# Sixteen 128-column products of the maxima made eight of 256 columns, and three steps of the even units reordered, in a two-layer cross-attention kernel on one core

## The reference

```python
def layer(x, ctx, Wq, Wk, Wv, Wo, bo):            # x (32,256,320), ctx (32,77,512)
    q, k, v = heads(x @ Wq), heads(ctx @ Wk), heads(ctx @ Wv)   # 20 heads of 16
    p = softmax(einsum('bhsd,bhld->bhsl', q, k) / sqrt(16))     # over the 77 keys
    return merge(einsum('bhsl,bhld->bhsd', p, v)) @ Wo + bo + x
x = layer(layer(x, ctx, L0...), ctx, L1...)
```

## Time and profile before

| what | value |
|---|---|
| times of three runs | 942.4, 946.02, 947.88 us; median 946.02 us |
| the profiled execution's own time | 937.91 us |
| its span (first to last instruction) | 936.1 us |
| TensorE busy, share of the span | 901.5 us, 96% |
| VectorE, ScalarE, GpSimd busy | 73%, 58%, 43% |
| mean granted TensorE clock | 0.998 of full |

### The profile page before, as it was taken

One profiled execution on the slowest core, in us unless ns is written; L12 is line 12 of the kernel. 1 busy time (PEld: TensorE's weight loads), 2 busy tenths in 40 slices (PEclk: granted clock), 3 DMA queues, 4 the chain that ended last, 5 costly groups with the idle time before them and its releaser, 6 DMA issues.

```text
span 936.1 us, 30582 instructions
## 1 busy us (share of the span) xinstructions
PE 901.5 (96%) x12766; PEld 692.7 (74%) x12766; DVE 686.5 (73%) x1223; ACT 540.1 (58%) x547; POOL 399.6 (43%) x227
## 2 busy tenths in 40 slices
PE   8899999999999999999899999999999999999897
PEld 5777877777787877777677787877878777777665
DVE  4875786866778776786867778686786868778566
ACT  4456565655556566566466556556565656656552
POOL 3424354533446254275543456354344625433323
PEclk9999999999999999999999999999999999999999
DMA  6213534545345544545455435444534544443442
GB/s 214 88 34 83 142 82 131 139 122 138 92 110 133 162 127 111 137 111 153 124 146 131 108 101 141 134 129 113 143 97 114 141 128 134 102 129 80 120 109 78
DMA packets 80537, 112.58 MB, mean 120 GB/s; under 512 B 21201, under 2 KB 37879, under 8 KB 80401
## 3 DMA queue, kind: packets, MB, share of 16 engines
q1 hardware_dynamic: 80400, 110.62, 44.1%
HBM read 60.24 MB, written 22.24 MB: 88 GB/s over the span
## 4 chain that ended last, share of the span: by engine, by line
PE 42%; DMA 20%; SPq 17%; DVE 10%; issue 6%; ACT 3%; POOL 1%; DVEq 0%; ACTq 0%; POOLq 0%
PE pR L305 16%; PE pR L430 8%; DMA X<-in_xT 7%; SPq L1387 6%; PE pA L377 5%; DMA X<-y 5%; PE pR L364 5%; DMA y<-X 4%; SPq L1394 3%; DMA out<-X 3%; SPq L1357 3%; ACT P L740 2%; PE pA L383 2%; DVE Oraw L1006 2%; SPq L1421 2%
## 5 line engine op out<-in xcount | busy, mean ns | idle before, releaser
L740 ACT ACTIVATE P<-pA 77x2048 f32<-77x2048 f32 x160 | 300.1, 1876 | 171.8 <-PE pA L383 171.5
L991 DVE TENSOR_REDUCE Mx<-pR 128x4 f32<-128x308 f32 (+1 forms) x480 | 258.8, 575 | 32.8 <-PE pR L364 29.8
L1250 POOL TENSOR_TENSOR On<-On,OS 128x1024 f32<-128x1024 f32 (+1 forms) x58 | 105.5, 1840 | 272.0 <-DMA OS<-rd 272.0
L305 PE MATMUL pR<-OS,Wo 128*128 128x512 f32 x638 | 168.9, 404 | 2.2 <-DVE OS L1047 1.4
L305 PE MATMUL pR<-XS,Wq 128*128 128x512 f32 x638 | 167.5, 402 | 2.6 <-POOL Wq L1236 1.5
L430 PE MATMUL pR<-P,VA 77*17 77x256 f32 x2480 | 157.0, 384 | 0.7 <-ACT P L740 0.3
L364 PE MATMUL pR<-KH,QH 32*128 32x154 f32 x1280 | 136.5, 292 | 19.1 <-ACT P L740 7.8
L364 PEld LDWEIGHTS pR<-KH,QH 32*128 32x128 f32 x1280 | 95.7, 184 | 78.1 <-issue 44.4
L377 PE MATMUL pA<-QH,KH 32*77 32x256 f32 x1280 | 145.1, 291 | 0.1
L305 PEld LDWEIGHTS pR<-XS,Wq 128*128 128x128 f32 x638 | 115.9, 189 | 29.4 <-POOL Wq L1236 1.9
L305 PEld LDWEIGHTS pR<-OS,Wo 128*128 128x128 f32 x638 | 114.1, 188 | 30.7 <-issue 3.8
(11 more groups left out here) (152 smaller groups left out, 1199.0 us busy)
## 6 DMA issues: line engine op xcount, KB each, us to landing
On<-Oraw SPq DMA_DIRECT2D x248, 64.0 KB, 2.6
OS<-rd SPq DMA_DIRECT2D x58, 256.0 KB
C<-in_cT SPq DMA_DIRECT2D x16, 616.0 KB, 7.9
X<-in_xT SPq DMA_DIRECT2D x16, 512.0 KB
y<-X SPq DMA_DIRECT2D x16, 512.0 KB, 4.1
X<-y SPq DMA_DIRECT2D x16, 512.0 KB
out<-X SPq DMA_DIRECT2D x15, 512.0 KB, 4.1
X<-in_xT SPq DMA_DIRECT2D x16, 256.0 KB
```

The costliest lines, as they stand in the source:

```text
L305: f = pe.matmul(p[:, :], W[:, k, c0:c0 + 128], S[:, s, :], start=(i == 0), stop=(i == len(pairs) - 1))
L740: act.activation(P[0:L, i % PR, :, :], pA[0:L, :, :], ACT.Exp, scale=float(D) ** -0.5).then_inc(p_done, 1)
L991: dve.tensor_reduce(Mx[:, :].rearrange("p (j i) -> p j i", j=4)[:, j:j + banks, i:i + 4], pR[:, bank:bank + banks, 0:2 * LK].rearrange("p ...
L1250: pool.tensor_tensor(On[rows, blocks, :], On[rows, blocks, :], recips(u, part).bitcast(F32), ALU.mult).then_inc(o_mul, 1)
```

## The change

There are three edits. The products of `less_maxima` take 256 columns instead of 128: `Mx` holds the two blocks of 128 tokens of a batch side by side (128 x 2 x 128), `max_rows` makes two transposes into one bank and copies 256 columns, `neg` has 10 columns, the reduction writes its outputs into the two blocks, and `run` has 10 steps instead of 12. In the even units ScalarE takes the exponential S(u, 1) ahead of `split_x(u + 2)`. And in all even units but 30, TensorE does K(w, 2) ahead of Q(u + 2, 2), with the half copies of ScalarE and the half sums of VectorE in the same order.

```diff
-NI = 20
+NI = 10
-        Mx = sb("Mx", [128, 128])
-        Mt = sb("Mt", [128, 128], F32R)
+        Mx = sb("Mx", [128, 2, 128])
+        Mt = sb("Mt", [128, 2 * 128], F32R)
@@ TensorE
-                pe.transpose(p[:, 0:128], Mx[:, :], ident[:, :]).then_inc(mt_pe, 1)
+                pe.transpose(p[:, 0:128], Mx[:, 0, :], ident[:, :])
+                pe.transpose(p[:, 128:256], Mx[:, 1, :], ident[:, :]).then_inc(mt_pe, 1)
-                def less_maxima(t, j):
-                    i = 8 * ms + 2 * t + p if ms < 2 else 16 + 2 * (t % 2) + t // 2
-                    return pe.matmul(pA[0:L, j, t * 128:t * 128 + 128], neg[32 * j:32 * j + 32, i:i + 1].broadcast_to([32, L]),
+                def less_maxima(h, j):
+                    i = 4 * ms + 2 * h + p if ms < 2 else 8 + h
+                    return pe.matmul(pA[0:L, j, h * SQ:h * SQ + SQ], neg[32 * j:32 * j + 32, i:i + 1].broadcast_to([32, L]),
                                      Mt[32 * j:32 * j + 32, :], start=False, stop=True, skip_group_check=True)
-                for step in range(12):
+                for step in range(10):
-                    if u is not None and step == 11:
+                    if u is not None and step == 9:
                         g.then_inc(s_pe, 1)
-                    if n is not None and step == 10:
+                    if n is not None and step == 8:
                         take_pair(second, 1)
-                        if 6 <= step < 10 and u is not None:
+                        if 6 <= step < 8 and u is not None:
                             less_maxima(step - 6, j)
-                        if step >= 10 and n is not None:
-                            f = tokens_by_keys(step - 10, j)
+                        if step >= 8 and n is not None:
+                            f = tokens_by_keys(step - 8, j)
+                    K(w, 2, 0)
                     Q(u + 2, 2, 3)
-                    K(w, 2, 0)
@@ ScalarE
-                act.activation(Mt[:, :], psum(slot["MX", u])[:, 0:128], ACT.Copy).then_inc(mt_copied, 1)
+                act.activation(Mt[:, :], psum(slot["MX", u])[:, 0:256], ACT.Copy).then_inc(mt_copied, 1)
+                        S(u, 1)
                         split_x(u + 2)
-                        S(u, 1)
+                    k_half_copy(w)
                     q_half_copy(u + 2)
-                    k_half_copy(w)
@@ VectorE
-                i = 8 * m + 4 * b
+                i = 4 * m + 2 * b
-                dve.tensor_reduce(Mx[:, :].rearrange("p (j i) -> p j i", j=4)[:, j:j + banks, i:i + 4],
-                                  pR[:, bank:bank + banks, 0:2 * LK].rearrange("p j (a k) -> p j a k", k=L),
+                dve.tensor_reduce(Mx[:, :, :].rearrange("p t (j i) -> p j t i", j=4)[:, j:j + banks, :, i:i + 2],
+                                  pR[:, bank:bank + banks, 0:2 * LK].rearrange("p j (t a k) -> p j t a k", t=2, k=L),
+                    k_sum(w)
                     q_sum(u + 2)
-                    k_sum(w)
```

More of the change, by code:

```diff
@@ L406, in run @@
                             keys_by_tokens(step, j)
-                        if 6 <= step < 10 and u is not None:
+                        if 6 <= step < 8 and u is not None:
                             less_maxima(step - 6, j)
-                        if step >= 10 and n is not None:
-                            f = tokens_by_keys(step - 10, j)
-                    if n is not None and step == 11:
+                        if step >= 8 and n is not None:
+                            f = tokens_by_keys(step - 8, j)
+                    if n is not None and step == 9:
                         f.then_inc(x_pe, 1)
@@ L1263, in _ @@
                 pool.memset(ones[:, p, D - D * p:2 * D - D * p], 0.0)
-            pool.memset(Mx[:, :], 0.0).then_inc(pads, 1)
+            pool.memset(Mx[:, :, :], 0.0).then_inc(pads, 1)
             pool.wait_ge(d_c, 16)
```

## The result

The changed kernel is slower by 0.65%. Its median is 949.12 us over 20 runs (944.02 to 954.98), that of the kernel before 944.36 us over 20 runs on the same chip (938.33 to 949.14); the ratio is 1.0065, with a 95% interval of 1.0043 to 1.0088. The forecast was 0.66% faster (939.8 of 946.0) in a range of 931 to 947, so the sign was missed, and the range by 2 us at its upper end. Forecast and measured change, -6.2 and +4.8 us, lie 11 us apart.

What follows compares the result with a forecast made beforehand. TensorE's own work was taken as the bound, busy 901.5 of 936.1 us. Wider products -4.5, transpose +2.4, the orders -2.5 and clock -1.6 sum to -6.2: 939.8 of 946.0 us, range 931 to 947.

Steps and rivals of the forecast that it cites:

- K ahead of Q: Even units: K(w, 2), 1.2 us, fills TensorE's 1.0 us wait for GpSimd before Q; moving half copies and sums costs nothing.
- the clock: TensorE's granted clock, 0.58 of full after a 1.42 us wait, recovers if that wait goes: -1.6 us (0 to -1.6).
- Wider products: Stages on TensorE: 256-column products save 0.035 us a stage in about 130 of 160, -4.5 us (0 to -7.4).
- The second transpose: TensorE: one more transpose costs 0.15 us, uncovered in 16 odd units, +2.4 us (+1.3 to +6.2).
- Exponential ahead of the rounding: ScalarE, even units: waits before stage 2 go; seven units gain 4.4 us, five others lose 0.8 in all.
- GpSimd's end: Unit 12: GpSimd's work on x ends at 388.77, before K ends at 388.93, so Q does not wait; margin 0.2 us.
- The wait of 1.75 us: In the unit with this wait there is no V(w, 2) to fill; TensorE waits for GpSimd, some 0.3 us stays won.
- Q of unit 14: GpSimd also forms Wq's rest; the chain starts 2.0 us later, K fills 1.2: +0.8 us (0 to +2.0).
- -4.4 - 0.3 + 0.8: Exponential first: seven units' waits -4.4 us, the 1.75 us wait's unit -0.3, five units with early x +0.8.
- The parts did not cancel: Rival: short products cost only their columns and a transpose 0.20 us in every unit; +2 us, about 946; chance 0.25.
- the slower rival: VectorE's reductions, output cut into two blocks, cost 0.15 us more each and become the bound; about 952; chance 0.08.
- Late transfers: Rival: x lands later in timed runs, waits twice as large, the reorder wins 5 us more; 934.5; chance 0.15.

Runs made afterwards that it cites:

- e3: Kernel before with only K(w, 2) moved ahead of Q(u + 2, 2), in the old banks; 961.41 us, 1.0157 of the kernel before.
- e4: Changed kernel with only the banks exchanged, K(w, 2) in bank 3 and Q(u + 2, 2) in bank 0; 937.45 us, 0.9899 of the kernel before.
- e9: Kernel before with only K(w, 2) ahead of Q(u + 2, 2) and their banks exchanged (3 and 0); 938.74 us, 0.9973 of the kernel before.
- e10: The same kernel as e4, all of the change with banks exchanged, timed again in another set; 935.39 us, 0.9935 of the kernel before.
- e5: Kernel before with only the exponential S(u, 1) ahead of the rounding of x; 961.36 us, 1.0180 of the kernel before.
- e2: Kernel before with only the wide products and their two transposes, all orders as before; 944.86 us, 0.9980 of the kernel before.
- e8: e4 with four more transposes a unit, whose results nobody reads; 941.34 us, 0.9976 of the kernel before.
- e11: Kernel before with both changes of order and the banks of K and Q exchanged, products narrow; 936.91 us, 0.9956 of the kernel before.
- e1: Changed kernel with Q(u + 2, 2) put back ahead of K(w, 2); wide products and exponential first stay; 953.53 us, 1.0086 of the kernel before.

## Why the prediction was wrong

**The step that failed** is this sentence of the part on K ahead of Q: "Moving the two half copies and half sums costs nothing: both lie beside PV and stage 3; if they came late, the maxima of stage 3 behind them would." It asked who is queued behind the half sums on VectorE, and not who waits for the bank that they free. In place of nothing the trace has 0.65 us in each even unit from 0 to 28, 9.8 us in 15 units. All that was needed stood in the code and in the earlier trace rows: bank 3 in the call of Q, the pair 2 and 3 in the call of stage 3, a copy of half a bank and two sums behind it, as V(w, 2) has them in the earlier trace rows, and only PV left between. e3 shows the wait without the other edits, and e4, e9 and e10 show it gone when Q lies in another bank.

**Its price is more than the waits.** e3 loses 17 us against e9, and its 15 waits on the half sum are 9.8 us of them. A second part is a collision. VectorE's `K_lo` of the third block comes after stage 3, and where it meets GpSimd's normalisation it is held up. In unit 12 of the changed kernel:

```profile
395.59 3.69 POOL L1252 TENSOR_TENSOR On<-On,OS 128x1024 f32<-128x1024 f32 x2 [4.78 <-DMA OS<-rd]
395.63 3.83 DVE L917 SCALAR_TENSOR_TENSOR KL<-Kt,mask,KH 128x154 fp32r<-128x154 f32 x2
...
399.38 0.79 DVE L993 TENSOR_REDUCE Mx<-pR 128x8 f32<-128x616 f32 x1
...
400.42 0.34 PE L366 MATMUL pR<-KH,QH 32*128 32x154 f32 x2 [2.06 <-DVE Mx L993]
```

The two instructions of line 917 take 2.54 and 1.37 us beside GpSimd's two of 2.40 and 1.33, where this form has a median of 0.37:

```profile
L917 DVE SCALAR_TENSOR_TENSOR KL<-Kt,mask,KH x32: 367/372/2536, 48.3 to 851.0; 128x154 fp32r<-128x154 f32 x32
```

The maxima behind them come late, and with them the banks of stage 4. GpSimd loses next to nothing: its pairs take 2.39 and 1.29 us where nothing meets them. The Trainium skill (SBUF — State Buffer, "SBUF: two separate sides") says that VectorE and GpSimd share a pair of ports under a lock held for the whole instruction, that a VectorE instruction with two inputs in SBUF needs it against a GpSimd instruction that reads SBUF, and that the one that starts second is blocked. The trace agrees: GpSimd's start first (395.59 against 395.63, 397.95 against 398.09), and each of line 917 ends 0.17 to 0.18 us after the one of line 1252 that it met.

The waits on these late maxima are 4.9 us in 3 places here and 4.7 in 4 in e3, against one of 2.0 before and none in e9 and e10 over the same stretch. They come with any delay in the middle of the unit and not with the bank wait alone: e5, which waits at Q instead, has 5.4 us in 4 places.

A third part could be the clock, which the prediction had as a gain, and here single profiles mislead. Two windows of the changed kernel, with the columns of the earlier trace rows:

```profile
458.50:468.00 9.50, 7.65 (x69) 6.12 (x62) 5.84 (x11) 4.31 (x5) 3.01 (x3) 0.64 0.28 86
904.80:917.00 12.20, 10.56 (x124) 5.79 (x125) 7.60 (x12) 4.86 (x6) 3.45 (x2) 0.63 0.23 70
```

Ahead of the first stand TensorE's waits of 1.69 us (Q in unit 14, at 451.73) and 0.65 us (bank 3, at 454.82), and within it one of 1.85. At 0.64 of full a part of the time is at 1.2 GHz: the eight products of line 306 from 463.45 on take 3.78 us, against 2.11 at full clock (425.16). By the granted clock of the records, the time at 1.2 GHz adds up to 21 us in the changed kernel's profiled execution, 25 in e3 and 24 in e5, but only 4 in that of before and 6 in e9 and in e10. That looks like a rule, but the other profiles break it: e2, without any of the new waits, has 28 us, and e4 has 14 where e10, the same kernel, has 6.

The timed runs say more, as each has its mean granted clock on record. Their mean is 0.9934 over the 20 runs of the changed kernel, and 0.9938 over the 21 runs of before in the first set (the 20 beside the changed kernel have none on record), so the clock does not explain why the change is slower. For e3 it may explain a part: 0.9895 over 6 runs against 0.9938 for before, where e9 has 0.9957 against 0.9950. A difference of 0.005 is some 9 us more at 1.2 GHz, and these cost at most half of it, some 5 us, an estimate from these means. Bank waits (9.8), late maxima (4.7) and clock (up to 5) together can make the 17 us between e3 and e9. How they divide is not shown, since no run has one without the others.

**Wider products: right mechanism, smaller.** A stage that nothing holds went from 1.367 us, the median before, to 1.32, 0.047 less. One of them, in unit 13, from its first product to the next operation:

```profile
423.84 0.34 PE L366 MATMUL pR<-KH,QH 32*128 32x154 f32 x2
...
425.16 2.11 PE L306 MATMUL pR<-XS,Wq 128*128 128x512 f32 x8
```

That is more than the 0.035 that were taken, but only in half the stages. Stages 0, 3 and 4 of the even units and 3 and 4 of the odd have it. Stage 1 of the even and stages 1 and 2 of the odd units stay at 1.39, stage 0 of the odd at 1.58: their second pair of banks is held by VectorE's `out` and `o_copy`. The "ordinary stage" of the earlier trace rows, 1.39 us, was itself a held one. So it is 80 stages times 0.047, -3.8 us, and not 130 times 0.035, -4.5. The 256-column products follow each other 0.117 apart, as expected. (The formula that the prediction took from the Trainium skill's "Back-to-back issue gap" is given there for the gap of an isolated product; for a stream in which each product has its weight load the section has about 81 ns at 128 columns, where the rows here have 0.07.)

**The second transpose: right, smaller.** In the timeline of the changed kernel:

```profile
469.07 0.27 PE L329 MATMUL pR<-ident,Mx 128*128 128x128 f32 x1
469.18 0.27 PE L330 MATMUL pR<-ident,Mx 128*128 128x128 f32 x1
469.38 0.43 PE L432 MATMUL pR<-P,VA 77*17 77x256 f32 x4
```

It costs 0.11 us and not 0.15, so 16 times 0.11 is +1.8 and not +2.4. In front of PV, where nothing waits, the next product came 0.20 us after the single transpose and comes 0.31 after the first of two. In front of V it came after 0.085 (369.44 to 369.53 before) and comes after 0.194; there the second transpose starts 0.165 after the first and V 0.03 behind it. The 0.19 of the earlier trace rows was the reading of one unit, 13, in which TensorE had just waited 0.18 us; thirteen of the fifteen places have 0.085. The two ends taken for the price, 0.08 and 0.20, enclosed it. The Trainium skill (TensorE: Matmul & The Clock Gate, "Part 4: PE-mode transpose") has about 275 ns for one inside a kernel. That agrees with how long each is in the records here (0.27), but it is not what one more costs: transposes that follow one another are 0.11 apart in e8. The net of both terms is -2.0 worked out, -1.9 in e2 (0.998) and -1.5 between e11 and e10. It was forecast as -2.1. None of the runs tells it from zero by its interval.

**Exponential ahead of the rounding, and GpSimd's end: right in the timeline.** 4.89 us after stage 1 (forecast 5.04), no wait on the exponential, GpSimd's end some 0.1 us before Q. The wait of 1.75 us was forecast to leave 0.3 of gain; in the changed kernel that place (842.32) waits 1.65 us for line 1060, so 0.1 stays. Q of unit 14 waits 1.69 against 1.50 and starts after K, as priced. In unit 0, K waits 1.03 for its bank, as priced too. e1 and e5 bear out that the exponential needs K in front: alone it costs 1.8%. What it brings with K in front is smaller than forecast: e11 and e9 differ by it alone and lie 1.8 us apart in their medians, which their intervals do not tell from nothing, where -4.4 - 0.3 + 0.8, -3.9, was worked out. In e11 2.2 us of waits ahead of stage 2 end with VectorE's `out(z, 0)` instead.

**The sum without the failed step.** e10 has every edit of the change, and only the bank numbers differ. Its ratio of 0.9935 is -6.1 us of 941.5; the forecast for the change was -6.2. Of this, the two orders alone (e11) give 0.9956, -4.1, where -2.5 and -1.6 were worked out. The interval of each is some 2 us to either side, so this agreement is better than the data can vouch for, and in part it is luck. The clock term, -1.6, is not borne out: the mean granted clock is 0.9954 over the 12 runs of e10 and 0.9950 over those of before in its set, worth at most 0.4 us. And e9, K first with exchanged banks and nothing else, is already 0.27% faster than before, 2.5 us, for which the prediction has no term; the reason stays open.

**The rivals.** The parts did not cancel: that case would have put e2 some 6 us above before, and e2 lies 0.1 us below it in the medians of its set, with 0.9947 to 1.0013 as the interval. The reductions stayed at 575 ns, so the slower rival failed as a mechanism, though its side was the right one. Late transfers are partly true: the profile of before had 7.8 us of waits on the exponential, e2 has 10.1, e9 10.5 and e3 12.2 with the same place of it, so that profile was a light one in this too. It changed little, as part of these waits then ended with line 1060 instead.

## What to carry to other kernels

When a product is moved, write down its bank, who asks for that bank next, and how long its release takes (here copy and sums, 1.6 us); the move is free only while that much work lies between. What is queued behind the releasing instruction is only half the question. If an order is wanted for other reasons, exchange the banks first: it costs nothing, and here it was the difference between +0.65% and -0.65%.

Before multiplying a gain by a count of stages, sort the stages by what ends them; a shorter stage gains nothing where its second pair of banks comes late. And where runs spread by over 1%, do not read a rule from one profiled execution of each kernel: by their profiles the clock seemed to tell the slow kernels from the fast ones, and by the means over the timed runs the changed kernel and the one before have the same.

## What the runs showed of the hardware that was not expected

One more transpose of 128 x 128 costs TensorE 0.11 us, in front of PV and in front of V, singly and in a row of four (0.44 us), though each lasts 0.27 in the records. Their starts need not show it: in front of V the second one starts 0.165 us after the first and the next product 0.03 after that.

A reduction that writes its outputs in two separate blocks, by one more dimension, takes the same 575 ns as one that writes a single block.

In a row group of 32 partitions a product of 256 columns follows at 0.117 us, two of 128 took 0.13 to 0.14; so halving the number of products at equal columns gave 0.047 us a stage where nothing else held it.

A VectorE instruction of 0.37 us with two inputs in SBUF took up to 2.54 us when a GpSimd instruction had started just before it, and ended 0.17 to 0.18 us after that one; GpSimd's own took 2.40 instead of 2.39.

A wait of 0.65 us in each of 15 units went with a loss of 17 us where its own sum was 9.8. Such collisions on VectorE are a second part; the clock may be a third.
